# FFN activations of a mixture-of-experts block: turned by VectorE and sixteen SBUF to SBUF transfers instead of by TensorE

## The reference, cut to what matters

```python
z = _layernorm(x)                      # 2048 tokens, D = 256
probs = softmax(z @ gate_w)            # E = 8 experts
expert_weights, expert_indices = top_k(probs, 2)      # then scaled to sum 1
for i in range(E):
    wi = jnp.where(expert_indices == i, expert_weights, 0.0).sum(-1)
    h = silu(z @ w1[i]) * (z @ w3[i])                 # F = 1024
    out = out + (h @ w2[i]) * wi[..., None]
x = x + out
```

## Time and profile before

| | us |
|---|---|
| runs | 494.84, 495.22, 1086.1 |
| median | 495.22 |
| span of the profiled execution | 492.8 |
| prologue (to the first up projection) | 119 |
| loop, steps 1 to 36 | 129.2 to 474.6 |
| TensorE busy, share of the span | 422.1, 86% |

### The profile page before, as it was taken

How to read it: one execution, slowest core, us unless ns; L and a number is a source line. 1 busy time by engine, 2 the same in 40 slices (tenths; PEclk the granted TensorE clock), 3 DMA queues, 4 the chain that set the end, 5 groups by cost and what they waited for, 6 DMA issues and landing times.

```text
span 492.8 us, 10407 instructions
## 1 busy us (share of the span) xinstructions
PE 422.1 (86%) x2557; PEld 365.9 (74%) x2558; DVE 263.6 (53%) x670; ACT 192.5 (39%) x334; POOL 169.9 (34%) x133
## 2 busy tenths in 40 slices
PE   0678984314999999999999999999999999999980
PEld 0556864313888889888888988888898888889870
DVE  7877869997454255433563564355356433653230
ACT  3446443301444246233542643354264334542230
POOL 5455434442023333322242333224233322532321
PEclk9979795555999999999999999999999999999995
DMA  6856885604415421541118118111811211121120
GB/s 196 297 179 206 272 268 157 200 1 139 161 23 160 149 32 32 203 105 23 30 21 287 32 21 283 32 26 21 287 32 21 32 30 23 21 32 32 21 32 11
DMA packets 33076, 50.92 MB, mean 103 GB/s; under 512 B 3335, under 2 KB 25095, under 8 KB 33063
## 3 DMA queue, kind: packets, MB, share of 16 engines
q1 hardware_dynamic: 24983, 38.44, 23.4%
q0 software_dynamic: 8080, 12.33, 12.8%
HBM read 39.36 MB, written 11.40 MB: 103 GB/s over the span
## 4 chain that ended last, share of the span: by engine, by line
PE 73%; DVE 7%; issue 2%; DMA 1%; POOL 1%; ACT 1%; ACTq 0%; POOLq 0%; DVEq 0%
PE bank L1312 64%; PE bank L1335 7%; PE bank L1319 2%; DVE ctx_sb L901 2%; DVE onehot_lo L986 1%; DVE rank L889 1%; DMA dg<-depool_rows,plugi 1%; PE bank L1266 1%; POOL dg L441 1%; DMA xblk<-z_rows,gidx 1%; PE bank L1191 0%; DVE batch L990 0%; POOL out L485 0%; DVE st L823 0%; DVE x_all L820 0%
## 5 line engine op out<-in xcount | busy, mean ns | idle before, releaser
L1312 PE MATMUL bank<-split,xT_hi 128*128 x592 | 166.8, 403 | 1.3 <-DVE xT_lo L1087 1.3
L1096 DVE TENSOR_TENSOR hmul<-gact,bank 128x512 f32<-128x512 f32 x74 | 50.9, 688 | 149.1 <-ACT gact L614 149.1
L485 POOL DMA_INDIRECT out<-yblk,itok x37 | 78.4, 2118 | 149.8 <-ACT yblk L621 138.2
L1312 PEld LDWEIGHTS bank<-split,xT_hi 128*128 128x128 f32 x592 | 106.9, 190 | 22.6 <-issue 1.9
L1312 PE MATMUL bank<-split,hT 128*128 (+1 forms) x888 | 115.4, 286 | 1.4 <-issue 0.8
L1312 PEld LDWEIGHTS bank<-split,hT 128*128 128x128 f32 x888 | 108.5, 191 | 2.1 <-issue 1.2
L614 ACT ACTIVATE gact<-bank 128x512 f32<-128x512 f32 x74 | 44.2, 598 | 158.9 <-PE bank L1312 158.8
L1312 PE MATMUL bank<-split,xT_lo 128*128 x296 | 93.7, 398 | 0.0
L477 POOL DMA_INDIRECT xblk<-z_rows,gidx x40 | 40.1, 1001 | 106.0 <-DVE gidx L1109 100.3
L321 DVE TENSOR_TENSOR split<-raw,split x21 | 48.1, 2293 | 37.6 <-ACT split L315 37.6
L1312 PEld LDWEIGHTS bank<-split,xT_lo 128*128 128x128 f32 x296 | 56.0, 189 | 13.5
(11 more groups left out here) (182 smaller groups left out, 332.4 us busy)
## 6 DMA issues: line engine op xcount, KB each, us to landing
raw<-in_L_ffn_w SPq DMA_DIRECT2D x24, 1024.0 KB, 8.0
ctx_sb<-in_ctx SPq DMA_DIRECT2D x4, 1024.0 KB, 6.4
x_all<-in_x SPq DMA_DIRECT2D x4, 512.0 KB, 8.3
depool_rows<-gact SPq DMA_DIRECT2D x4, 512.0 KB, 3.0
out<-x_all SPq DMA_DIRECT2D x4, 512.0 KB, 5.5
z_rows<-z SPq DMA_DIRECT2D x4, 512.0 KB, 3.9
xblk<-z_rows,gidx POOLq DMA_INDIRECT x40, 2.8
out<-yblk,itok POOLq DMA_INDIRECT x37, 4.7
```

The source lines that it names most:

```text
L485: pool.indirect_dma_start(out[:, :], bass.IndirectOffsetOnAxis(ap=itok[:, q:q + 1], axis=0), yblk[:, q, :], None, compute_op=ALU.add).then ...
L1096: dve.tensor_tensor(hmul[:, cols], gact[:, cols], p_lin[part][:, :], ALU.mult)\
L1312: mm = pe.matmul(out_, xp, w_, start=start and n == 0, stop=stop and n == 2)
```

## The change

The transposes of h on TensorE go, but for the last block. In their place:
- DVE transposes within squares of 32 by 32 (`turn`), each half of `hmul` in one instruction of 128x512, into `swap_in`.
- SP then issues 16 transfers from SBUF to SBUF (`exchange`), one for each pair of quadrants (a, b) of 32 partitions: 32 partitions of 1 KB each, 32 KB in one transfer, 512 KB in all. They bring square (a, b) to partition quadrant b, in `swap_out`.
- ACT makes the high part and DVE the low part of hT from `swap_out`, in one instruction of 128x1024 each instead of two of 128x512.
- The down projection in step i is that of block i-2, `y` and `meta` likewise, and the scatter on POOL too. On ACT `y` now comes ahead of the splits. Steps 0 and 1 stand outside the loop. After the last step two blocks are left instead of one.
- `up` on PE gets waits on h of the step before, since no transposes order them now. Smaller: one more column in the table, three zero fills instead of two on POOL, `dg`'s space shared with `swap_in`.

The core of the diff; lines left out are marked:

```diff
+Q = 32
+NQ = P // Q
+EXCHANGE = 16 * NQ * NQ
...
+            def exchange(i, q):
+
+                sp.wait_ge(s["swap_ready"], 2 * (i + 1))
+                settle(sp)
+                if after(i, 2):
+                    sp.wait_ge(s["hTlo_ready"], i - 1)
+                    settle(sp)
+                for a in range(NQ):
+                    for b in range(NQ):
+                        sp.dma_start(swap_out[b * Q:(b + 1) * Q, q, a], swap_in[a * Q:(a + 1) * Q, q, b])\
+                          .then_inc(swapped[q], 16)
+
             def step(i, q, half, word):
+                exchange(i, q)
                 with sp.If(word & F_LOAD):
...
             def add_rows(i, q):
-                pool.wait_ge(s["y_ready"], i + 2)
+                pool.wait_ge(s["y_ready"], i + 3)
...
             def hT(i, q, half):
-                act.wait_ge(s[f"th{half}_done"], i + 1)
-                act.activation(hT_hi[:, q, half * KF // 2:(half + 1) * KF // 2], p_hT[half][:, :], ACT.Copy)\
-                   .then_inc(s[f"hT{half}hi_ready"], 1)
+
+                act.wait_ge(swapped[q], EXCHANGE * half)
+                act.activation(hT_hi[:, q].rearrange("p k (a t) -> p a k t", a=NQ), swap_out[:, q], ACT.Copy)\
+                   .then_inc(s["hThi_ready"], 1)
...
             def step(i, q, half, word):
-                later = not isinstance(i, int) or i > 0
                 silu(i, 0)
-                if later:
-                    hT(i - 1, 1 - q, 1)
                 xT(i + 1, 1 - q)
                 silu(i, 1)
-                hT(i, q, 0)
+                if after(i, 1):
+                    hT(i - 1, 1 - q, half + q)
+                if after(i, 2):
+                    y(i - 2, q)
 
                 with act.If(word & F_CHUNK):
                     e = expert(word)
...
-                if later:
-                    y(i - 1, 1 - q)
...
+            def turn(i, q, half, part):
+
+                dve.wait_ge(s[f"h{part}_done"], i + 1)
+                if after(i, 2):
+                    dve.wait_ge(swapped[q], EXCHANGE * half)
                 ks = slice(part * KF // 2, (part + 1) * KF // 2)
-                dve.wait_ge(s[f"hT{part}hi_ready"], i + 1)
+                dve.transpose(swap_in[:, q, :, ks, :].rearrange("p b k t -> p k b t"),
+                              hmul[:, part * HALF:(part + 1) * HALF].rearrange("p (k b t) -> p k b t", b=NQ, t=Q))\
+                   .then_inc(s["swap_ready"], 1)
+
+            def hT(i, q):
+
+                dve.wait_ge(s["hThi_ready"], i + 1)
+                dve.tensor_tensor(hT_lo[:, q].rearrange("p k (a t) -> p a k t", a=NQ), swap_out[:, q],
+                                  hT_hi[:, q].bitcast(f32).rearrange("p k (a t) -> p a k t", a=NQ), ALU.subtract)\
+                   .then_inc(s["hTlo_ready"], 1)
...
             def step(i, q, half, word):
-                later = not isinstance(i, int) or i > 0
                 h(i, 0)
-                if later:
-                    hT(i - 1, 1 - q, 1)
-                    meta(i - 1, 1 - q)
                 xT(i + 1, 1 - q)
+                turn(i, q, half, 0)
                 next_index(i + 3, 1 - q, half + q + 1)
...
                 h(i, 1)
-                hT(i, q, 0)
+                turn(i, q, half, 1)
+                if after(i, 1):
+                    hT(i - 1, 1 - q)
+                if after(i, 2):
+                    meta(i - 2, q)
...
             def step(i, q, half, word):
...
                 pe.wait_ge(s["lo_ready"], expert(word) * 3 + 2)
+                if after(i, 1):
+                    pe.wait_ge(s["h0_done"], i)
 
                 up(slot, q, 0)
...
-                if later:
-                    hT(i - 1, 1)
                 xT(i + 1, 1 - q, half + q)
 
+                if after(i, 1):
+                    pe.wait_ge(s["h1_done"], i)
                 up(slot, q, 1)
-                hT(i, 0)
-                if later:
-                    down(i - 1, 1 - q, expert_before(word), (word >> PREV_BIT) & 1)
+                if after(i, 2):
+                    down(i - 2, q, expert_before(word), (word >> PREV_BIT) & 1, s["hTlo_ready"], i - 1)
 
             def drain(i, q):
-                hT(i, 1)
-                down(i, q, E - 1, (E - 1) & 1, by_halves=True)
+
+                hT_last(i, 0)
+                hT_last(i, 1)
+                word = step_word(pe, i + 1)
+                down(i - 1, 1 - q, expert_before(word), (word >> PREV_BIT) & 1, s["hTlo_ready"], i)
+                down(i, q, E - 1, (E - 1) & 1, s["drainlo_ready"], 2)
```

More of the change, by code:

```diff
@@ L186, in build @@
             ln_p = sb("ln_p", [P, 3, NBC], i32, early)
-        dg = sb("dg", [P, 2, TPB, D], f32)
+        with ExitStack() as early:
+            dg = sb("dg", [P, 2, TPB, D], f32, early)
+        swap_in = sb("swap_in", [P, 2, NQ, KF, Q], f32)
+        swap_out = sb("swap_out", [P, 2, NQ, KF, Q], f32)
         onehot_hi = sb("onehot_hi", [P, NBC, TPB], bf16)
@@ L255, in build @@
         blk_in = [sem(f"blk_in{q}") for q in range(2)]
+        swapped = [sem(f"swapped{q}") for q in range(2)]
         block = stack.enter_context(nc.Block())
@@ L289, in over_steps, with after, blocks_less_two, at_end @@
         def over_steps(eng, body):
-            body(0, 0, 0, step_word(eng, 0))
+            for i in range(2):
+                body(i, i, 0, step_word(eng, i))
             with eng.Fori(0, STEP_PAIRS) as pair:
-                word = step_word(eng, pair * 2 + 1)
+                word = step_word(eng, pair * 2 + 2)
                 with eng.If(word & F_RUN):
-                    body(pair * 2 + 1, 1, pair, word)
-                    word = step_word(eng, pair * 2 + 2)
+                    body(pair * 2 + 2, 0, pair + 1, word)
+                    word = step_word(eng, pair * 2 + 3)
                     with eng.If(word & F_RUN):
-                        body(pair * 2 + 2, 0, pair + 1, word)
-        def block_count(eng):
+                        body(pair * 2 + 3, 1, pair + 1, word)
+        def after(i, n):
+            return not isinstance(i, int) or i >= n
+        def blocks_less_two(eng):
             eng.wait_ge(s["blocks_ready"], 1)
[L302 to L309, removed]
+            return eng.value_load(blocks_i[:, :], min_val=E - 2, max_val=BLOCKS - 2)
+        def at_end(eng, less_two, drain):
+            with eng.If(less_two & 1):
+                drain(less_two + 1, 0)
+            with eng.If((less_two + 1) & 1):
+                drain(less_two + 1, 1)
         def split_hi(act, raw3, m):
@@ L395, in step @@
                     raw_load(sp, e + 3, (e + 1) & 1, s["raw_ready"])
+            less_two = blocks_less_two(sp)
             over_steps(sp, step)
+            for q in range(2):
+                sp.wait_ge(swapped[q], ((less_two + 3 - q) >> 1) * EXCHANGE)
+                settle(sp)
         @block.gpsimd
@@ L424, in pad_out @@
                 pool.wait_ge(s["pad_ready"], 1)
[L425 to L427 removed]
+                for a, n in ((0, P // 2), (P // 2, P // 4), (P * 3 // 4, P // 4)):
+                    pool.dma_start(out[T + a:T + a + n, :], zeros[0:n, :]).then_inc(s["added_rows"], 16)
             def pow1(b):
@@ L1150, in drain @@
             def drain(i, q):
-                hT(i, q, 1)
+                hT_last(i, q, 0)
+                hT_last(i, q, 1)
+                meta(i - 1, 1 - q)
                 meta(i, q)
-            blocks = block_count(dve)
+            less_two = blocks_less_two(dve)
             over_steps(dve, step)
-            at_end(dve, blocks, drain)
+            at_end(dve, less_two, drain)
         @block.tensor
```

80 lines of the change are left out of this document (43 added, 37 removed).

## The result

The changed kernel takes 598.29 us (median of 4 runs, 597.48 to 598.93), the kernel before 495.03 beside it. The ratio is 1.2106 [1.2081, 1.2131]. Forecast were 509 us and a range of 496 to 534: the direction was right, the size far out.

What follows compares the result with a forecast made beforehand. The prediction took TensorE to bound the kernel at 9.56 us a step. Loop +0.2, weight loads +10 and end +4 made +14 on 495.2, so 509 us, range 496 to 534.

Steps and rivals of the forecast that it cites:

- What is added on SP: On SP's queue: 16 issues a step at 0.47 us (0.42 to 0.60) plus 1.0 of own work, 8.5 us.
- the loop's 345.6: All 36 loop steps: 21 behind splits at 10.35 us and 15 at 8.55, against 345.4 before, +0.2.
- Where it lands: ACT and DVE waits tie block i's exchange to block i+2's: two steps take 16.3 us, 20.0 with a split.
- 10.35 for steps behind a split: In the loop: average TensorE step behind a split, with waits for DVE's low part of xT.
- Weight loads: In five steps the exchange queues behind 3 MB and lands late, scatter slowed too: 2 us each, 10 us (0 to 20).
- The end: After the loop: two blocks left; low part, y between the downs and the last scatter add about 4 us.
- ACT waits for the transfers: Expected sign in the profile after: ACT idle in front of hT, waiting for DMA into swap_out; no size.
- Rival 4: On DVE: slow squares, 1.2 us per `turn`, add 0.5 per step, 18 us: 527; chance 0.11.
- Rival 3: On SP: 16 issues at 0.55 each make SP the bound, 9.8 us every step: 534, or 520 at 0.52; chance 0.13.
- SP issuing without a pause: Sign in the profile after that would show SP to be the bound; no size.
- Rival 2: In the loop: exchange hidden, TensorE stays the bound, 40 us saved, about 460; chance 0.07, whole or in part.
- The clock: On TensorE: clock still granted in full, as it stays busy over 85% of the loop.

Runs made afterwards that it cites:

- to-DRAM kernel: The changed kernel with its 16 transfers, same bytes and partitions, sent to a DRAM tensor instead of `swap_out`: 528.72 us, ratio 1.0698.

## Why the prediction failed, step by step

- **"What is added on SP": the term that failed.** Issue 0.635 instead of 0.47, above the upper bound of 0.60, and SP's own work 1.5 instead of 1.0, which I had read from steps without an exchange. SP's step is 11.65, so the loop's 345.6 become 36 x 11.65 = 419.4: 74 of the 89 us by which the time exceeds the forecast. The end is 6.4 more, the weight loads 6 (16 for 10). Of the last 3, 2.5 are how the loop is cut: the forecast counts 345.4 for the 36 steps of before, and between the first and the last high part of xT, where the changed kernel is measured, they are 342.9. The to-DRAM kernel shows what the dearer issue costs by itself, 69.6 us; SP is no longer always the last there and waits 33.5 us for turns. The row chosen was the nearest in pattern, static and back to back, but not in kind: no transfer from SBUF to SBUF was in the trace, and a price for it could only have been bounded by a wider range.
- **"Where it lands": the loop through two steps.** No chain that was read is bound by it. In the changed kernel SP is above it (order altered: 3 us). Where SP is quick enough another loop takes over, which the forecast did not draw: `meta`, `y`, split, h, turn, low part, `meta`, one step long, 9.77 us, no transfer in it. That is so with four issues, and also with sixteen at the forecast's own price: there most steps with a split are 9.8 to 10.0, and in one of them DVE's low part (405.92) starts as its second turn (405.18, 0.71 us) ends, with the high part just over. My 10.35 for steps behind a split was near it by luck, for another reason.
- **"Weight loads": 10 us forecast.** The mechanism was another one. In the changed kernel the last of the 16 issues behind the load at 302.13 lands in 2.1 us, as forecast without one (315.08 to 317.23): the 9.7 us of issues before it outlast the load. What a load costs is SP's time, 2.5 each for the load and 0.3 to 1.0 for slower issues behind it, 16 us. With short exchanges the bytes show as a late landing, 8.3 us, and at the forecast's issue price they cost 12.7 us in all. Of the 20 us between 528.7 and 509, 12.7 are these bytes. The other 7 (516.0 against 509, small loads still holding up a step) I haven't taken apart: SP's 0.5 a step, TensorE's 8.68 and the delay of the issues all lie in it.
- **"The end": 4 forecast, 10.4 measured.** With four issues it is 4.8 (the last high part of xT to the end is 28.5 us there, 23.7 before). The rest is the last exchange at 0.635 an issue, and the last but one down projection at the lower clock level (5.14 for 2.97; with four issues 2.94).
- **Right:** turn 0.71 (0.69), high 1.06 (1.05), low 1.23 (1.2), landing: last issue 315.08, `hT` on ACT 317.23 on the timeline, 2.1 us (2.0). ACT waits for the transfers. Rival 4 fell with the turn; the Trainium skill, "VectorE: DVE Perf Modes", section "The three transpose paths", gives 311 ns for 128x128 in bf16, and the estimate of 1.24 from it was too high: the trace has 706 ns for four times that in float32.
- **Rival 3** was the mechanism, "SP issuing without a pause" its sign, and both are in the trace. It had a chance of 0.13 and ended at 534, because 0.55 was the most I gave an issue there, although my own upper bound was 0.60; that makes 10.6 a step, 36 more than the sum, 545, and the range stopped short of it. By its own formula 0.635 and 1.5 make 11.65 a step and 583 us; the missing 15 are the loads, the end and the cut of the loop above.
- **Rival 2**, that with a short exchange TensorE bounds and about 460 is the result, holds where its condition does, but only once `meta` and the splits are moved too: 465.7 with four wide issues, where from the fourth on every step is 8.7 us. Without that, 496. The chain of the kernel with 465.7:

```profile
PE 72%; DVE 10%; issue 6%; DMA 5%; POOL 3%; ACT 2%; DVEq 0%; POOLq 0%; ACTq 0%; SPq 0%
```

- **The clock** did not stay full. That was wrong as a forecast of a row (and the row of before already ends in a 5, which my reading "in full from slice 10 on" passed over); in the loop TensorE is off the chain, at the end it is about 2 us.

The Trainium skill, "DMA: Bandwidth & Descriptors", section "Issuing engines are not separate DMA queues", has the issue as usually small beside the transfer. This trace disagrees at 32 KB: one issue takes 0.59 of the 2.1 us to the landing, and since issues follow one another while the transfers overlap, sixteen are 10.2 us of issues with one landing behind them.

## What to carry over

A transfer split into many small ones is paid on the queue that issues them; count them per step, and multiply by the price of the same kind (source and destination), or widen the range if the trace has none. Moving work off the busiest engine is worth only the distance to the next limit, and here there were three in a row: SP's issues, the order of waits in two engines, and the queue that the weight loads share. Going from 16 issues to 5 (through DRAM), with the splits and `meta` ahead of the waits and the loads on another queue, made of the 598 us a kernel of 479.7. TensorE holds the largest share of its chain again, and its steps away from loads are 8.7 us; the transfers still hold 14%:

```profile
PE 42%; DMA 14%; DVE 13%; issue 8%; ACT 4%; ACTq 2%; SPq 1%; POOL 1%; DVEq 1%; POOLq 0%
```

## What the runs showed of the hardware

- An issue from SP costs 0.635 us from start to start for SBUF to SBUF, and 0.47 for SBUF to DRAM with the same bytes and partitions. Between 4 KB and 32 KB it makes no difference (591 ns each), between 32 and 128 partitions almost none (591 and 601).
- Behind 3 MB on its own queue SP issues more slowly for a while: single issues up to 1.52 us (SBUF to SBUF) and 2.02 (to DRAM), and none above 0.63 behind the same three loads cut to 32 columns.
- SP and ACT issue at the same time and hardly slow each other: 602 and 612 ns medians with two queues, 591 for SP alone.
- Four transfers of 128 KB behind 3 MB on their own queue land after 7.9 to 8.5 us, one of 512 KB after 9.8 to 12.7; with the 3 MB on ACT's queue the longest for the 512 KB in a chain of waits was 7.3, but the reads back beside the first load took 10.3.
- A float32 turn in squares of 32 by 32 runs at the rate of a plain product: 706 ns for 128x512 against 679 for h.
